# Three batches' roots and normalised tiles of the first attention on GpSimd, its bias additions two pairs later

## The chip, the cores and the metric

The kernel runs on one core of a Trainium2 chip. A core has five engines with a queue each, which meet only through semaphores: TensorE (PE) multiplies, VectorE (DVE) and ScalarE (ACT) read and write PSUM and SBUF, GpSimd (POOL) works on SBUF alone, and SyncE (SP) issues most transfers. The metric is the device time of one execution in microseconds, the median of the runs.

## What is computed

The reference is two transformer layers, each an attention and a feed-forward part with a layer norm after each. The change lies in the first attention, which has 4 batches of 512 rows and 256 columns, 16 heads of 16 columns, and in the norm behind it:

```python
B, S, H = hidden_states.shape
qkv = jnp.einsum('bsh,hf->bsf', hidden_states, w_qkv) + b_qkv
...
q_rot = q_rot * cos + _rotate_half(q_rot) * sin
k_rot = k_rot * cos + _rotate_half(k_rot) * sin
...
scores = jnp.einsum('bhqd,bhkd->bhqk', q, k)
scores = jnp.where(causal, scores, jnp.float32(-jnp.inf).astype(scores.dtype))
probs = jax.nn.softmax(scores, axis=-1)
attn = jnp.einsum('bhqk,bhkd->bhqd', probs, v)
...
return jnp.einsum('bsh,hf->bsf', attn, w_out) + b_out
```

```python
x = _layernorm(x + _L0_attn_ref(x, L0_attn_w_qkv, L0_attn_b_qkv, L0_attn_w_out, L0_attn_b_out), axis=-1)
```

`_layernorm` subtracts the row's mean and divides by the root of its variance plus 1e-5. Everything is float32; products are made of a high and a low part of each operand.

## The kernel before

`attention0` holds one program for each engine. Batches come one after the other in *entries*: `entry(0, "first")`, two of `"loop"` (i = 1, 2) and `entry(3, "last")`. An entry has 8 *pairs* of heads (p = 0 to 7) with 4 *rows of tiles* each (r = 0 to 3), so 32 slots (p, r). Entry i works on the heads of batch i; beside that it prepares the heads of batch i + 1 and finishes batch i - 1: it projects its output, adds the residual, normalises the sum and transposes the result for the next stage. Nothing is scheduled by a planner. The order of each engine is written by hand in tables of slots: `WORK_AT` (the uses of one PSUM bank, `work`), `HIGH_AT` and `LOW_AT` (the high and low parts of the stacked heads), `VALUES_AT`, `BIAS_TILE_AT` and `KEEP_TILE_AT`.

In a slot (p, r) of a loop entry:

- TensorE makes the score products from which row maxima are taken, two pairs ahead (`max_pass`, L824, of 128 (r + 1) columns), the score products for the exponentials (L835), in half of the slots a group of value products (`value_pass`, L848), and one use of the work bank: a projection (L871), a turn of stacked heads (`turn_stack`, L878), a part of the output projection (L887) or a transpose (L943). `max_pass` has two banks; each product waits until VectorE has reduced what was in its bank two products ago.
- VectorE reduces both `max_pass` banks (L1104), adds the bias to projections (L1153), and does the rest of the PSUM reading that falls to it. The norm of batch i - 1 is a generator, `normalise`, of which two steps are taken in each slot from (4, 0): statistics (L86, L91) in (4, 0), nine steps of a root by iteration on 128x4 numbers (L96 to L121), and behind them in (5, 1), all at once, the four tiles `xn = (rsum - mean) * y` (L158).
- ScalarE makes the exponentials (L695), copies turned heads from PSUM (L682, L688) and makes the high parts of stacks (`stack_high`, L674 and L676).
- GpSimd clears the upper triangle of the exponentials (`select`, L579), rotates projected heads (`rotate`, L564 to L568), copies values (L572), and makes the low parts of stacks (`stack_low`, L585 and L587). It adds the output bias to the residual tiles of batch i (`residual_bias`, L606, four tiles at (5, 1), (5, 2), (5, 3), (6, 0)) and keeps the normalised tiles plus a bias (`keep`, L599, four tiles at (6, 2) to (7, 1)).

GpSimd takes its work strictly in this order: in one slot `stack_low`, `select`, `rotate`, `values`, `keep`, `residual_bias`. The turns of stacked heads on TensorE wait for `stack_low`; two of them are in pair 5: half 2, tile 2 at (5, 1), whose low part is made at (5, 0), and half 2, tile 3 at (5, 3), whose low part is made at the head of (5, 3). The latter's heads are rotated at (5, 0). The normalised tiles are first read by the transposes at (6, 2) and by `keep` there; the residual tiles with their bias by the additions at (3, 0) of the next entry.

The last entry has no `rotate`, and no stacks of half 2. It projects nothing for a next batch; its slots have the products of two weight matrices instead (L923, L929), and VectorE has their preparation.

A root of the same kind is already worked out on GpSimd, in the next stage (`pool_rstd`, L135 to L146, called at L1657): twelve operations, each behind a wait for the one before.

Of the kernel before, what the change touches and what calls it, by code (L numbers as in the profile page):

```python
# [127 lines left out]

def pool_rstd(pool, chain, mv, var, t, u, y):

    def step(ins):
# [4 lines left out]
    step(pool.tensor_scalar(y.bitcast(I32), var[:, :].bitcast(I32), -0.5, float(RSQRT_MAGIC), ALU.mult, ALU.add))
    step(pool.tensor_tensor(t[:, :], y, y, ALU.mult))
    step(pool.tensor_tensor(t[:, :], t[:, :], var[:, :], ALU.mult))
    step(pool.tensor_scalar(t[:, :], t[:, :], -1.0, STEP_2[1], ALU.mult, ALU.add))
    step(pool.tensor_tensor(y, y, t[:, :], ALU.mult))  # L140
    step(pool.tensor_tensor(t[:, :], y, y, ALU.mult))
    step(pool.tensor_tensor(t[:, :], t[:, :], var[:, :], ALU.mult))
    step(pool.tensor_scalar(u[:, :], t[:, :], STEP_3_T, None, ALU.subtract))
    step(pool.tensor_tensor(t[:, :], t[:, :], u[:, :], ALU.mult))
    step(pool.tensor_scalar(t[:, :], t[:, :], STEP_2[0] ** 4, 5.0, ALU.mult, ALU.add))
    step(pool.tensor_tensor(y, y, t[:, :], ALU.mult))  # L146
# [146 lines left out]
BIAS_TILE_AT = ((5, 1), (5, 2), (5, 3), (6, 0))  # L293
# [67 lines left out]
def attention0(nc, A, g, top):  # L361
# [444 lines left out]
    def _(pe):  # L806
# [85 lines left out]
        def use_work(i, when, kind, arg):  # L892
# [38 lines left out]
            else:  # L931
# [7 lines left out]
                else:  # L939
                    pe.wait_ge(s["v_norm"], i + 1)  # L940
# [128 lines left out]
    def _(v):  # L1069
        chain = Chain(v, s["v_chain"])  # L1070
        for name in ("work_read", "ex_read", "a_out", "v_norm", "g_x1"):
            v.sem_inc(s[name], 1)
# [179 lines left out]
        def entry(i, when):  # L1252
# [4 lines left out]
            for n, (p, r) in enumerate(slots):  # L1257
# [28 lines left out]
                if (p, r) == (4, 0) and when != "first":  # L1286
                    norm = normalise(i, when)
# [1365 lines left out]
```

## Time and profile before

| | us |
|---|---|
| median of 3 runs | 1067.95 (1067.92 to 1068.65) |
| span of the profiled execution, first to last instruction | 1067.0 |
| TensorE busy | 1004.4 |
| VectorE busy | 747.8 |
| ScalarE busy | 612.4 |
| GpSimd busy | 375.2 |
| first attention: second entry, pair 0 to pair 7 | 97.0 to 161.8 |
| first attention: third entry | 161.8 to 226.6 |
| first attention: last entry | 226.6 to about 307 |

The two loop entries take 64.8 us each and are alike almost to the hundredth: what is seen in the second entry is found again 64.8 us later. "Busy" of TensorE is the time in which a matmul is under way, and matmuls overlap, so that a short idle time of TensorE in a row is more than it looks. In a row of a timeline the number in brackets is the time for which the engine stood idle before it, with what ended it. "PEclk" is the granted TensorE clock as a share of 2.4 GHz: 0.50 is 1.2 GHz.

### The profile page before, as it was taken

The page shows a single profiled execution, that of the slowest core. Times are in us where ns is not written, and L with a number is a line of the kernel's source. Part 1 is how long each engine was busy: PE and PEld are TensorE (multiplying, and loading weights), DVE is VectorE, ACT ScalarE, POOL GpSimd, SP SyncE. Part 2 cuts the span into 40 slices and gives each one's busy share as a digit, 9 for nine tenths or more (in the row PEclk, how much of TensorE's full clock was granted, in tenths as well). Part 3 has the DMA queues.
Part 4 walks back from the last instruction along what each step waited for, and adds up shares of the span by engine and source line. Part 5 has one row for each costly group of instructions (what it writes and reads, how often), then busy time and mean ns, then how long its engine had stood idle before and what let it go on. Part 6 is the DMA issues. An engine that isn't in the chain of part 4 may idle for free.

```text
span 1067.0 us, 18308 instructions
## 1 busy us (share of the span) xinstructions
PE 1004.4 (94%) x6627; PEld 836.8 (78%) x6627; DVE 747.8 (70%) x2042; ACT 612.4 (57%) x1177; POOL 375.2 (35%) x725
## 2 busy tenths in 40 slices
PE   6999999999998898889999999999999999999995
PEld 5555556556667897778989999998999999899995
DVE  5666777777639778967557767666776766677646
ACT  5566667664368576545556665455666545566640
POOL 3444464562121474454622233222223322222600
PEclk9899999999999899999999999999999999999998
DMA  7000000022210001021201010010101001010101
GB/s 244 25 2 21 3 22 21 23 60 80 61 46 4 1 6 36 1 100 61 79 1 40 1 40 22 19 41 1 40 1 41 27 14 40 1 41 1 49 32 40
DMA packets 29234, 36.91 MB, mean 35 GB/s; under 512 B 1780, under 2 KB 26584, under 8 KB 29144
## 3 DMA queue, kind: packets, MB, share of 16 engines
q1 hardware_dynamic: 24872, 31.28, 9.2%
q10 hardware_dynamic: 4272, 4.46, 1.4%
q8 instruction: 53, 0.87, 0.3%
q14 instruction: 37, 0.30, 0.1%
HBM read 31.40 MB, written 4.20 MB: 33 GB/s over the span
## 4 chain that ended last, share of the span: by engine, by line
PE 54%; DVE 5%; ACT 1%; POOL 1%; issue 1%; DMA 1%; SPq 0%; DVEq 0%; POOLq 0%; ACTq 0%
PE ps L1894 25%; PE ps L1877 24%; PE ps L1849 2%; PE ps L1767 1%; PE ps L1818 1%; DVE ln_stats L86 1%; DMA mlp_b<-L_ffn_LN_B 1%; DVE ln_stats L2256 0%; ACT xn L2016 0%; ACT x_b L2037 0%; DVE att L2339 0%; PE ps L1809 0%; DVE xT_l L2298 0%; PE ps L1720 0%; DVE ln_mv L91 0%
## 5 line engine op out<-in xcount | busy, mean ns | idle before, releaser
L2115 ACT ACTIVATE G<-ps,bias_col 128x512 f32<-128x512 f32 x192 | 135.5, 706 | 186.3 <-PE ps L1877 176.8
L1894 PE MATMUL ps<-w_h,G_h 128*128 128x256 f32 x736 | 208.2, 283 | 0.0
L1894 PE MATMUL ps<-w_h,G_l 128*128 128x256 f32 x736 | 207.9, 282 | 0.0
L1894 PE MATMUL ps<-w_l,G_h 128*128 128x256 f32 x736 | 207.8, 282 | 0.0
L2387 DVE TENSOR_TENSOR G_l<-G,G_h 128x512 fp32r<-128x512 f32 x192 | 155.1, 814 | 60.0 <-ACT G_h L2116 60.0
L1696 POOL TENSOR_TENSOR x_a<-xn,mlp_g 128x1024 f32<-128x1024 f32 x20 | 67.6, 3378 | 344.7 <-DVE xn L2417 344.7
L695 ACT ACTIVATE probs<-ps 128x512 f32<-128x512 f32 (+3 forms) x256 | 98.3, 440 | 108.4 <-PE ps L835 108.0
L1877 PE MATMUL ps<-xT_h,w_h 128*128 128x512 f32 x384 | 152.0, 396 | 1.1 <-issue 1.1
L1877 PE MATMUL ps<-xT_h,w_l 128*128 128x512 f32 x384 | 150.6, 392 | 0.0
L1877 PE MATMUL ps<-xT_l,w_h 128*128 128x512 f32 x384 | 150.3, 391 | 0.0
L1894 PEld LDWEIGHTS ps<-w_h,G_h 128*128 128x128 f32 x736 | 139.9, 190 | 0.7
L1894 PEld LDWEIGHTS ps<-w_h,G_l 128*128 128x128 f32 x736 | 140.3, 191 | 0.0
L1894 PEld LDWEIGHTS ps<-w_l,G_h 128*128 128x128 f32 x736 | 139.5, 190 | 0.8
L1104 DVE CUSTOM_DVE_ANT_0 ps<-ps,q_mask 128x128 f32<-128x128 f32 (+3 forms) x256 | 120.5, 511 | 25.9 <-PE ps L824 24.3
L2116 ACT ACTIVATE G_h<-ps,bias_col 128x512 fp32r<-128x512 f32 x192 | 135.0, 703 | 0.0
L2401 DVE TENSOR_TENSOR rsum<-ps,x_a 128x1024 f32<-128x1024 f32 x23 | 28.2, 1225 | 105.5 <-PE ps L1894 105.5
L579 POOL TENSOR_SCALAR_AFFINE_SELECT probs<-probs 128x256 f32<-128x256 f32 x128 | 54.8, 428 | 103.8 <-ACT probs L695 103.6
L1877 PEld LDWEIGHTS ps<-xT_h,w_h 128*128 128x128 f32 x384 | 72.1, 188 | 16.2 <-issue 1.5
L1877 PEld LDWEIGHTS ps<-xT_h,w_l 128*128 128x128 f32 x384 | 72.1, 188 | 15.6
L1877 PEld LDWEIGHTS ps<-xT_l,w_h 128*128 128x128 f32 x384 | 72.2, 188 | 15.0
L824 PE MATMUL ps<-heads_T 64*128 64x128 f32 (+3 forms) x256 | 69.5, 420 | 9.8 <-DVE top_score L1104 8.9
L2381 DVE TENSOR_TENSOR xT_l<-hs,xT_h 128x512 fp32r<-128x512 f32 x40 | 77.0, 1952 | 2.3 <-ACT xT_h L2101 1.2
(303 smaller groups left out, 2125.0 us busy)
## 6 DMA issues: line engine op xcount, KB each, us to landing
w_raw<-L_ffn_W_T SPq DMA_DIRECT2D x12, 1024.0 KB, 5.2
hs<-L_attn_hidden_states SPq DMA_DIRECT2D x8, 512.0 KB, 4.1
x_kept<-hs SPq DMA_DIRECT2D x4, 512.0 KB, 3.2
w_raw<-x_kept SPq DMA_DIRECT2D x2, 1024.0 KB, 5.4
out<-xn SPq DMA_DIRECT2D x3, 512.0 KB, 2.9
w_raw<-L_ffn_ent_w_T SPq DMA_DIRECT2D x1, 1024.0 KB, 10.3
w_raw<-L_ffn_ent_pw SPq DMA_DIRECT2D x1, 1024.0 KB, 12.7
heads_T<-neg_rows SPq DMA_DIRECT2D x64, 2.0 KB
```

Of the source, the lines that this page charges most:

```text
L579: pool.affine_select(diagonal, diagonal, [[0, 2], [1, P]], ALU.is_ge, 0.0, base=0, channel_multiplier=-1).then_inc(s["g_sel"], 1)
L695: act.activation(probs[:, p % 2, o, OFF[j]:OFF[j] + COLS[j]], ps[:, score_bank(r, o), 0:COLS[j]], ACT.Exp).then_inc(s["a_exp"], 1)
L824: pe.matmul(ps[:, o, 0:(t + 1) * P], heads_T[rows, p // UP, 0, p % UP, t * P:(t + 1) * P], heads_T[rows, p // UP, 1, p % UP, 0:(t + 1) * P ...
L1104: v.tensor_tensor_reduce(ps[:, o, 0:(t + 1) * P], ps[:, o, 0:(t + 1) * P], q_mask[:, S - (t + 1) * P:S], 1.0, MASKED, ALU.add, ALU.max, to ...
L1696: pool.tensor_tensor(g.x_a[:, rows, :], xn[:, b % 2, :, :], bcast(g.mlp_g[:, i, :], 1, [P, RT, D]), ALU.mult).then_inc(feed["g_mul"], 1)
L1877: mm = pe.matmul(ps[:, hidden_bank(i, n), :], w[:, c, f * P:(f + 1) * P], x[:, b, c, :], start=(k == 0), stop=(k == 5))
L1894: mm = pe.matmul(ps[:, 4 + t // 2, (t % 2) * D:(t % 2 + 1) * D], x[b % 2][f][:, t * P:(t + 1) * P], w2_chunk(w, f), start=(k == 0), stop=( ...
L2115: act.activation(G32[n % 4], bank, ACT.Gelu, bias=bias)
L2116: act.activation(G_h[b % 2][f], bank, ACT.Gelu, bias=bias).then_inc(feed["a_g"], 1)
L2381: v.tensor_tensor(g.xT_l[:, b, c, :], src, g.xT_h[:, b, c, :].bitcast(F32), ALU.subtract).then_inc(feed["v_T"], 1)
L2387: v.tensor_tensor(G_l[b % 2][f], G32[n % 4], G_h[b % 2][f].bitcast(F32), ALU.subtract).then_inc(feed["v_gl"], 1)
L2401: v.tensor_tensor(g.rsum[:, :, :], ps[:, 4:6, :].rearrange("p a (b c) -> p (a b) c", c=D), g.x_a[:, b * RT:(b + 1) * RT, :], ALU.add).then ...
```

## The change

The root and the four tiles of batches 0, 1 and 2 move from VectorE to GpSimd. VectorE's generator is left with the statistics (`moments`), whose end is told by a semaphore of its own, `v_moments`. GpSimd takes four of the twelve root operations in each of (4, 1), (4, 2), (4, 3), behind `select` and ahead of `rotate`, and one tile in each slot of pair 5. The four bias tiles move from (5, 1), (5, 2), (5, 3), (6, 0) to (6, 0), (6, 1), (7, 2), (7, 3). The semaphore of the finished tiles is named `x1_normed` in place of `v_norm`; its waits stand where they stood. The norm of batch 3, after the last entry, stays on VectorE.

```diff
+POOL_ROOT_STEPS = 12
+def pool_rstd_steps(pool, chain, mv, var, t, u, y):
+    chain.step(pool.tensor_scalar(var[:, :], mv[:, :, 1], EPS, VAR_FACTOR, ALU.add, ALU.mult))
+    yield
+    chain.settle()
+    chain.step(pool.tensor_scalar(y.bitcast(I32), var[:, :].bitcast(I32), -0.5, float(RSQRT_MAGIC),
+                                  ALU.mult, ALU.add))
+    yield
...
 def pool_rstd(pool, chain, mv, var, t, u, y):
+    for _ in pool_rstd_steps(pool, chain, mv, var, t, u, y):
         chain.settle()
...
-BIAS_TILE_AT = ((5, 1), (5, 2), (5, 3), (6, 0))
+BIAS_TILE_AT = ((6, 0), (6, 1), (7, 2), (7, 3))
+ROOT_AT = ((4, 1), (4, 2), (4, 3))
+NORM_TILE_AT = ((5, 0), (5, 1), (5, 2), (5, 3))
...
+        def x1_root(i):
+            pool.wait_ge(s["v_moments"], i)
+            yield from pool_rstd_steps(pool, chain, g.lnw["mv"], g.lnw["var"], g.lnw["t"], g.factors[:, 0, 0, :],
+                                       g.lnw["y"][:, :])
+        def x1_tile(i, t):
+            if t == 0:
+                chain.settle()
+                wait(pool, s["a_nT"], KC * (i - 1))
+            ins = pool.tensor_scalar(xn[:, 0, t, :], g.rsum[:, t, :], g.lnw["mv"][:, t, 0:1], g.lnw["y"][:, t:t + 1],
+                                     ALU.subtract, ALU.mult)
+            if t == RT - 1:
+                ins.then_inc(s["x1_normed"], 1)
...
                     select(i, p, r)
+                    if when != "first" and (p, r) in ROOT_AT:
+                        for _ in range(POOL_ROOT_STEPS // len(ROOT_AT)):
+                            next(root)
+                    if when != "first" and (p, r) in NORM_TILE_AT:
+                        x1_tile(i, NORM_TILE_AT.index((p, r)))
...
-        def normalise(i, when):
...
+        def moments(i, when):
+            v.wait_ge(s["work_read"], WORK.number(i, when, ("out", 1)) + 1)
...
+                ins = v.bn_aggr(g.lnw["mv"][:, k, :], g.lnw["stats"][:, k, :])
+            ins.then_inc(s["v_moments"], 1)
```

VectorE, second entry, slots (5, 1) and (5, 2), before (L1104 are the reductions of the maxima, L121 the last step of the root, L158 the tiles):

```order
L1104 ISA ps,top_score<-ps,q_mask 128x256 [waits p_max]
L1104 ISA top_score 128x1
L1104 ISA ps,top_score<-ps,q_mask 128x256 [waits p_max]
L1104 ISA top_score 128x1
L121 SCALAR_TENSOR_TENSOR ln_y<-ln_t,ln_y 128x4 [waits v_chain]
L158 TENSOR_SCALAR xn<-rsum,ln_mv,ln_y 128x256 [waits g_x1,v_chain]
L158 TENSOR_SCALAR xn<-rsum,ln_mv,ln_y 128x256 x3
L1104 ISA ps,top_score<-ps,q_mask 128x384 [waits p_max]
```

The same place now (L1156 are the reductions):

```order
L1156 ISA ps,top_score<-ps,q_mask 128x256 [waits p_max]
L1156 ISA top_score 128x1
L1156 ISA ps,top_score<-ps,q_mask 128x256 [waits p_max]
L1156 ISA top_score 128x1
L1156 ISA ps,top_score<-ps,q_mask 128x384 [waits p_max]
```

Nothing stands between the reductions of (5, 1) and those of (5, 2) any more; nine small steps and four tiles are gone from slots (4, 1) to (5, 1).

GpSimd, second entry, from the end of (5, 0) to the low parts at the head of (5, 3), before (`val` is the copy of values, `hs` the residual tiles):

```order
L572 COPY val<-qkv 128x8x16
L579 AFFINE_SELECT probs<-probs 128x2x128 [waits a_exp]
L606 TENSOR_TENSOR hs<-hs,b_out 128x256 [waits xres_in]
L579 AFFINE_SELECT probs<-probs 128x2x128 [waits a_exp]
L572 COPY val<-qkv 128x8x16
L606 TENSOR_TENSOR hs<-hs,b_out 128x256
L585 TENSOR_TENSOR q_stack<-qkv,q_stack 128x8x16 [waits a_stack]
L587 TENSOR_TENSOR k_stack<-qkv,k_stack 128x8x16
```

Now, from the tile of (5, 0):

```order
L651 TENSOR_SCALAR xn<-rsum,ln_mv,ln_y 128x256 [waits g_chain]
L594 TENSOR_TENSOR turned<-qkv,rope 128x64 [waits g_rope,work_read]
L595 TENSOR_TENSOR turned<-qkv,rope 128x16x2
L596 TENSOR_TENSOR turned<-qkv,rope 128x16x2
L598 TENSOR_TENSOR qkv<-turned 128x8x2x4 [waits g_chain]
L602 COPY val<-qkv 128x8x16
L609 AFFINE_SELECT probs<-probs 128x2x128 [waits a_exp]
L651 TENSOR_SCALAR xn<-rsum,ln_mv,ln_y 128x256
L609 AFFINE_SELECT probs<-probs 128x2x128 [waits a_exp]
L651 TENSOR_SCALAR xn<-rsum,ln_mv,ln_y 128x256
L602 COPY val<-qkv 128x8x16
L615 TENSOR_TENSOR q_stack<-qkv,q_stack 128x8x16 [waits a_stack]
```

A tile of the norm stands in place of each of the two bias tiles, and one more stands ahead of the rotation of (5, 0).

GpSimd, second entry, slots (4, 1) and (4, 2), now:

```order
L609 AFFINE_SELECT probs<-probs 128x2x128 [waits a_exp]
L134 TENSOR_SCALAR ln_var<-ln_mv 128x4 [waits v_moments]
L137 TENSOR_SCALAR ln_y<-ln_var 128x4 [waits g_chain]
L141 TENSOR_TENSOR ln_t<-ln_y 128x4 [waits g_chain]
L144 TENSOR_TENSOR ln_t<-ln_t,ln_var 128x4 [waits g_chain]
L594 TENSOR_TENSOR turned<-qkv,rope 128x64 [waits g_rope,work_read]
L595 TENSOR_TENSOR turned<-qkv,rope 128x16x2
L596 TENSOR_TENSOR turned<-qkv,rope 128x16x2
L598 TENSOR_TENSOR qkv<-turned 128x8x2x4 [waits g_chain]
L609 AFFINE_SELECT probs<-probs 128x2x128 [waits a_exp]
L147 TENSOR_SCALAR ln_t<-ln_t 128x4 [waits g_chain]
L150 TENSOR_TENSOR ln_y<-ln_y,ln_t 128x4 [waits g_chain]
```

Before, the rotation followed `select` at once, and nothing but a `select` stood in (4, 2). TensorE, ScalarE and SyncE issue the same instructions in the same order as before.

## Rows read from the trace of the kernel before

**Rows 1.** Waits, 130 to 146 us: who waited for whom, total us, times, longest.

```profile
PEld ps L824 <- DVE top_score L1104: 3.1, 5, 1.9
PE ps L824 <- DVE top_score L1104: 1.0, 1, 1.0
```

**Rows 2.** Timeline of TensorE, first entry (start us, us, instruction, idle before).

```profile
68.00 0.39 PE L824 MATMUL ps<-heads_T 64*128 64x256 f32 x2
...
74.01 0.33 PE L824 MATMUL ps<-heads_T 64*128 64x128 f32 x2
...
76.52 0.54 PE L878 MATMUL ps<-ident_r,k_stack 128*128 128x128 f32 x4
...
80.70 0.50 PE L878 MATMUL ps<-ident_r,k_stack 128*128 128x128 f32 x4 [0.58 <-POOL k_stack L587]
...
81.48 0.33 PE L824 MATMUL ps<-heads_T 64*128 64x128 f32 x2
...
84.05 0.39 PE L824 MATMUL ps<-heads_T 64*128 64x256 f32 x2
```

**Rows 3.** Timeline of TensorE, the same slots of the second entry.

```profile
130.23 0.38 PE L824 MATMUL ps<-heads_T 64*128 64x256 f32 x2
...
136.25 0.41 PE L824 MATMUL ps<-heads_T 64*128 64x128 f32 x2
...
138.97 0.51 PE L878 MATMUL ps<-ident_r,k_stack 128*128 128x128 f32 x4
...
142.88 1.01 PE L824 MATMUL ps<-heads_T 64*128 64x512 f32 x2 [0.99 <-DVE top_score L1104]
...
144.29 0.54 PE L878 MATMUL ps<-ident_r,k_stack 128*128 128x128 f32 x4
...
145.09 0.47 PE L824 MATMUL ps<-heads_T 64*128 64x128 f32 x2
...
149.19 0.39 PE L824 MATMUL ps<-heads_T 64*128 64x256 f32 x2
```

**Rows 4.** Timeline of VectorE, second entry, slot (5, 1).

```profile
140.30 2.00 DVE L158 TENSOR_SCALAR xn<-rsum,ln_mv,ln_y 128x256 f32<-128x256 f32 x4
```

**Rows 5.** Busy time by stretch: us, PE, PEld, DVE, ACT, POOL, PEclk, DMA share, GB/s.

```profile
141.70:145.10 3.40, 2.40 (x26) 1.38 (x22) 3.29 (x11) 1.47 (x5) 2.63 (x7) 1.00 0.00 0
145.10:148.50 3.40, 3.40 (x16) 1.72 (x16) 0.63 (x5) 1.94 (x4) 1.10 (x2) 0.50 0.01 2
```

**Rows 6.** Waits of GpSimd, 131.9 to 143.0 us.

```profile
POOL probs L579 <- ACT probs L695: 2.0, 3, 1.4
...
POOL turned L564 <- DVE qkv L1153: 0.7, 2, 0.4
```

**Rows 7.** Timeline of GpSimd, second entry, slots (5, 2) and (5, 3).

```profile
142.41 0.72 POOL L606 TENSOR_TENSOR hs<-hs,b_out 128x256 f32<-128x256 f32 x1
143.09 0.46 POOL L585 TENSOR_TENSOR q_stack<-qkv,q_stack 128x128 fp32r<-128x128 f32 x1
143.50 0.46 POOL L587 TENSOR_TENSOR k_stack<-qkv,k_stack 128x128 fp32r<-128x128 f32 x1
```

**Rows 8.** GpSimd, single lines (minimum/median/maximum ns); then groups, 300 to 560 us.

```profile
L137 POOL TENSOR_TENSOR norm_t<-norm_scale x19: 197/199/702, 354.8 to 511.3; 128x4 f32<-128x4 f32 x19
L1668 POOL TENSOR_SCALAR hs<-rsum,norm_scale,norm_shift x16: 556/564/1606, 469.0 to 521.0; 128x256 f32<-128x256 f32 x16
...
L1668 POOL TENSOR_SCALAR hs<-rsum,norm_scale,norm_shift 128x256 f32<-128x256 f32 x16 | 12.7, 808 | 0.7 <-POOL norm_shift L1660 0.7
...
L138 POOL TENSOR_TENSOR norm_t<-norm_t,norm_var 128x4 f32<-128x4 f32 x19 | 4.7, 246 | 1.5
```

**Rows 9.** Last entry: TensorE in its timeline; then GpSimd's waits, 269 to 293 us.

```profile
260.50 0.62 PE L824 MATMUL ps<-heads_T 64*128 64x512 f32 x2
...
290.59 1.02 PE L824 MATMUL ps<-heads_T 64*128 64x512 f32 x2 [1.12 <-DVE top_score L1104]
...
POOL probs L579 <- ACT probs L695: 23.2, 7, 4.9
```

More of the change, by code:

```diff
@@ L126 @@
 STEP_3_T = 10.0 / (3.0 * STEP_2[0] ** 2)
+POOL_ROOT_STEPS = 12
[7 more added lines that the diff above has]
+    chain.settle()
+    chain.step(pool.tensor_tensor(t[:, :], y, y, ALU.mult))
+    yield
+    chain.settle()
+    chain.step(pool.tensor_tensor(t[:, :], t[:, :], var[:, :], ALU.mult))
+    yield
+    chain.settle()
+    chain.step(pool.tensor_scalar(t[:, :], t[:, :], -1.0, STEP_2[1], ALU.mult, ALU.add))
+    yield
+    chain.settle()
+    chain.step(pool.tensor_tensor(y, y, t[:, :], ALU.mult))
+    yield
+    chain.settle()
+    chain.step(pool.tensor_tensor(t[:, :], y, y, ALU.mult))
+    yield
+    chain.settle()
+    chain.step(pool.tensor_tensor(t[:, :], t[:, :], var[:, :], ALU.mult))
+    yield
+    chain.settle()
+    chain.step(pool.tensor_scalar(u[:, :], t[:, :], STEP_3_T, None, ALU.subtract))
+    yield
+    chain.settle()
+    chain.step(pool.tensor_tensor(t[:, :], t[:, :], u[:, :], ALU.mult))
+    yield
+    chain.settle()
+    chain.step(pool.tensor_scalar(t[:, :], t[:, :], STEP_2[0] ** 4, 5.0, ALU.mult, ALU.add))
+    yield
+    chain.settle()
+    chain.step(pool.tensor_tensor(y, y, t[:, :], ALU.mult))
+    yield
@@ L139, in pool_rstd @@
[L139 to L146, printed above, removed]
@@ L1238, in prepare, with normalise_last @@
                 yield
-        def normalise(i, when):
-            if when == "after":
-                v.wait_ge(s["v_tail"], 2 * KC)
-            else:
-                v.wait_ge(s["work_read"], WORK.number(i, when, ("out", 1)) + 1)
-            yield from layernorm_steps(v, chain, g.lnw, g.rsum, xn[:, 0, :, :], s["v_norm"],
-                                       (s["g_x1"], i))
+        def moments(i, when):
+            v.wait_ge(s["work_read"], WORK.number(i, when, ("out", 1)) + 1)
+            for k in range(RT):
+                ins = v.bn_stats(g.lnw["stats"][:, k, :], g.rsum[:, k, :])
+            chain.step(ins)
+            yield
+            chain.settle()
+            for k in range(RT):
+                ins = v.bn_aggr(g.lnw["mv"][:, k, :], g.lnw["stats"][:, k, :])
+            ins.then_inc(s["v_moments"], 1)
+            yield
+        def normalise_last():
+            v.wait_ge(s["v_tail"], 2 * KC)
+            layernorm(v, chain, g.lnw, g.rsum, xn[:, 0, :, :], s["x1_normed"], (s["g_x1"], B))
         PREPARE_AT = ((1, 2), (1, 3), (2, 0), (2, 1), (2, 2), (2, 3), (3, 2), (3, 3), (4, 0), (5, 1), (5, 3), (6, 1),
@@ L1286, in entry @@
                 if (p, r) == (4, 0) and when != "first":
-                    norm = normalise(i, when)
+                    norm = moments(i, when)
                 next(norm, None)
@@ L1363, in _ @@
                             x_res[:, 2 * half:2 * half + 2, :], ALU.add).then_inc(s["v_tail"], 1)
-        for _ in normalise(B, "after"):
-            pass
+        normalise_last()
         square(v, g, chain, 0)
```

22 lines of the change are left out of this document (9 added, 13 removed).

## The prediction

> **What bounds the kernel now.** The change touches only the first attention, so I read that stage, and first its waits [rows 1]. Between 130 and 146 us, pairs 4 and 5 of the second entry, TensorE's largest wait is for VectorE's maxima: its weight loads stand for 3.1 us, and the matmuls themselves for 1.0 us at one place. Then I read the timelines. The first entry does the same pairs without a norm on VectorE and without bias tiles on GpSimd, so it is the control for both. Pair 4 takes 6.01 us there, from 68.00 to 74.01 [rows 2], and 6.02 us in the second entry, from 130.23 to 136.25 [rows 3]: the root's small steps on VectorE cost nothing there. Pair 5 takes 7.47 us there, from 74.01 to 81.48 [rows 2], and 8.84 us here, from 136.25 to 145.09 [rows 3]: 1.37 us more. That is where the four tiles run in one piece of 2.00 us [rows 4], with the reductions of (5, 2) behind them and TensorE's next product behind those, idle for 0.99 us at 142.88 [rows 3].
>
> More follows. In the 3.4 us of that idle time TensorE is busy for 2.40 us, and in the next 3.4 us its granted clock is 0.50, that is 1.2 GHz [rows 5]. Slot (6, 0) then takes 4.10 us, from 145.09 to 149.19 [rows 3], against 2.57 us in the first entry [rows 2]: 1.53 us for the clock. So up to 2.9 us per loop entry hang on the tiles' place. The third entry repeats all of this.
>
> The rows to read next are those of the engine that gets the work. In the first entry, with VectorE free, TensorE still waits 0.58 us for GpSimd's low part at (5, 3), the row at 80.70 [rows 2]. GpSimd has no slack at that point even without norm or bias. In the second entry the same turn starts at 144.29 [rows 3], and its low part is done at 143.96 (143.50 plus 0.46) [rows 7]: 0.33 us to spare, and only because TensorE is late.
>
> **The change part by part, loop entries.** VectorE loses nine small steps and four tiles; the statistics stay. By the control that is worth 1.37 us of pair 5, if nothing takes its place.
>
> GpSimd gains, ahead of the low part of (5, 3): twelve root steps and three tiles (5, 0) to (5, 2), less the two bias tiles that leave (5, 1) and (5, 2). A step on 128x4 numbers has a median of 0.20 us [rows 8]. Each stands behind a wait for the one before, 0.08 us (1.5 us of idle time over 19, in the row of L138) [rows 8]; in groups of four that wait is met 9 times. 12 x 0.20 + 9 x 0.08 = 3.1 us. A tile of this form on GpSimd has a median of 0.56 us [rows 8], so three are 1.7 us; two bias tiles at 0.72 [rows 7] are 1.4 us. Together 3.4 us more work. Against it stands the time in which GpSimd waits on this stretch: 2.0 us for exponentials and 0.7 us for projections, 2.7 us [rows 6]. All of these waits can be filled, since what they wait for doesn't depend on GpSimd's lateness by a us. The remainder is 0.7 us. Independent neighbours overlap a little: two low parts of 0.46 us start 0.41 us apart [rows 7]; some six added instructions of that kind take 0.3 us off. So the low part ends 0.4 to 0.7 us later, at 144.3 to 144.6, the turn follows by about 0.1 us, and TensorE is at (5, 3)'s turn 0.1 to 0.4 us **later** than before, not earlier. The low part of (5, 1) is late in the same way, with all twelve root steps ahead of it; that wait lies within the later one and is not added. I take +0.2 us: nearer to the overlapped end, because most of GpSimd's rows show such overlap. The wait for the maxima goes, and the wait for GpSimd is what comes next; the 1.37 us are not gained.
>
> TensorE's idle time doesn't go away either, it moves: the pair would run in 7.5 us and takes 9.0. So I take the stretch at half clock to stay, 0 for it; the other end is -1.5 us per entry.
>
> What lies behind pair 5: the last tile is issued in (5, 3), some 0.6 us behind a `select`, and the transposes that need it are two and a half slots later, so they don't wait: 0. The bias tiles add one each to (6, 1), (7, 2) and (7, 3), 0.7 us each. No one waits for them before (3, 0) of the next entry, and behind them in GpSimd's queue are `select`s, whose value products come two slots later, and the low part at (7, 3); I count 0. Without that cover the last one would cost its 0.7 us. No DMA is moved, and SyncE's queue is as before. TensorE's new wait has ScalarE and VectorE behind it, which then have less to do. Two loop entries: 2 x 0.2 = +0.4 us.
>
> **Last entry.** It has no rotations and no stacks of half 2, and its slots are long: GpSimd waits 23.2 us for exponentials between 269 and 293 us [rows 9]. The root and tiles fit into that several times over, and no low part hangs on them. TensorE's idle time of 1.12 us at 290.59 goes [rows 9], and with it the stretching of the two products there, 1.02 us against 0.62 us for the same form at 260.50 [rows 9]: 1.5 us. VectorE's next piece, a weight matrix, may keep back a tenth or two. I take -1.4 us, between 0 (if ScalarE's exponentials hold the end of the entry) and -1.5.
>
> **Sum.** +0.4 - 1.4 = -1.0 us. The profiled span of 1067.0 us becomes 1066.0. The runs' median stands 0.95 us above the span of the profiled execution, which lies around it, and that is kept: **1067.0 us**, 0.1% below 1067.95.
>
> **Rivals.** (a) *GpSimd keeps up* and each loop entry falls to the control: -2 x 1.37 - 1.4 = -4.1 us, 1063.8 us, and with both half-clock stretches gone 1060.8 us. For it: GpSimd is busy only about half the time of the stage. Against it: the 0.58 us at 80.70 without any of this work [rows 2].
>
> (b) *The clock*: GpSimd takes over the bound as forecast, but the idle time, now split between (5, 1) and (5, 3), no longer brings the fall to 1.2 GHz in one entry or in both. -1.0 - 1.5 = -2.5 us, 1065.4 us, or 1063.9 us. Against it: the idle time at (5, 3) should be over the 0.99 us that came with the fall before.
>
> (c) *GpSimd's instructions run longer among VectorE's*, and the kernel gets slower. In the next stage the tile's mean is 0.81 us against a median of 0.56, and a step's 0.25 against 0.20 [rows 8]. At the means a loop entry gets 3 x 0.25 + 12 x 0.05 = 1.3 us longer, all of it on the path, as GpSimd has no slack left: 2 x 1.5 - 1.4 = +1.6 us, 1069.6 us. If the longer wait also brings a second stretch at half clock, +1.5 us more each, 1071 to 1072.6 us. It turns the sign once a loop entry loses more than 0.7 us.
>
> The Trainium skill speaks for (c): its page GPSIMD Engine Reference, section 8. Key points, holds that "for elementwise work, the DVE is structurally ~2× faster" and that GpSimd contends for SBUF with VectorE instructions of two SBUF inputs. By it a tile would take about 1.0 us here, 1.3 us more per loop entry, and the time would come out near that of (c). The trace disagrees in size: 2.00 us for four on VectorE [rows 4] and a median of 0.56 us for one on GpSimd [rows 8] are a factor of 1.1.
>
> **Chances.** Forecast 0.52 (its own range 1066.2 to 1068.8, with both ends of the loop term and of the last entry); (a) 0.08; (b) 0.20; (c) 0.14; and 0.06 that later stretches at half clock, which shift against the program by a us, add or take one, 1.5 us, more often as a gain here. A measurement tells apart about 0.2%, 2.1 us. Faster by more: (a), (b) and the last case, 0.34. Slower by more: the greater part of (c), 0.12. Between: 0.54. The range from 1063.5 to 1070.0 leaves out the far ends of (a) and (c).
>
> **What would show it.** Right: in the second entry VectorE's reductions of (5, 1) and (5, 2) stand next to each other; TensorE's wait at (5, 3) names GpSimd's `k_stack`, over 1 us long; the start of (6, 0) is within 0.5 us of 145.09; the clock is at 0.50 right behind it; the last entry has no 1.12 us of idle time. Wrong: pair 5 of 7.5 to 8 us in a loop entry means that GpSimd had the room (the count of its free time is at fault); one over 9.7 us, that its steps or tiles cost more than their medians. A clock of 1.00 in (6, 0) is (b).

## The result, and the profile after

The changed kernel takes 1084.42 us, the median of 4 runs (1083.1 to 1084.73), against 1067.93 us for the kernel before, also 4 runs. The ratio is 1.0152, with a 95% interval of 1.0138 to 1.0166: 16.5 us slower. The forecast was 1067.0 us with a range that ended at 1070.0 us, so it was wrong. The profiled execution of after has a span of 1082.7 us, 15.7 us over the 1067.0 us of before, and the account below is made between these two.

**Where the pair's time went.** TensorE's timeline of the second entry answers to [rows 3]. L876 is the product for the maxima, L930 a turn of stacked heads; they were L824 and L878.

```profile
135.06 0.33 PE L876 MATMUL ps<-heads_T 64*128 64x128 f32 x2
...
138.36 0.52 PE L930 MATMUL ps<-ident_r,k_stack 128*128 128x128 f32 x4 [0.86 <-POOL k_stack L617]
...
140.69 0.62 PE L876 MATMUL ps<-heads_T 64*128 64x512 f32 x2
...
145.50 0.50 PE L930 MATMUL ps<-ident_r,k_stack 128*128 128x128 f32 x4 [3.54 <-POOL k_stack L617]
...
146.43 0.47 PE L876 MATMUL ps<-heads_T 64*128 64x128 f32 x2
...
156.88 0.73 PE L876 MATMUL ps<-heads_T 64*128 64x128 f32 x2
```

Pair 5 takes 11.37 us (135.06 to 146.43), where it took 8.84 us. The wait for VectorE's maxima before the 128x512 product is gone: the row at 140.69 has no bracket and takes 0.62 us instead of 1.01 us. In its place TensorE stands idle for 0.86 us at (5, 1) and for 3.54 us at (5, 3), both times for GpSimd's low part. Pair 6 takes 10.45 us (146.43 to 156.88), where it took 9.27 us (145.09 to 154.36). The third entry is the same to a tenth.

GpSimd's timeline of the same place answers to [rows 7]. Two steps of the root in (4, 1) come first, then three tiles (L651) and the low part (L617):

```profile
132.21 0.20 POOL L137 TENSOR_SCALAR ln_y<-ln_var 128x4 int32<-128x4 int32 x1
132.49 0.20 POOL L141 TENSOR_TENSOR ln_t<-ln_y 128x4 f32<-128x4 f32 x1
...
138.57 1.24 POOL L651 TENSOR_SCALAR xn<-rsum,ln_mv,ln_y 128x256 f32<-128x256 f32 x1
...
141.47 1.23 POOL L651 TENSOR_SCALAR xn<-rsum,ln_mv,ln_y 128x256 f32<-128x256 f32 x1
...
143.05 1.22 POOL L651 TENSOR_SCALAR xn<-rsum,ln_mv,ln_y 128x256 f32<-128x256 f32 x1
...
144.89 0.46 POOL L617 TENSOR_TENSOR k_stack<-qkv,k_stack 128x128 fp32r<-128x128 f32 x1
```

The steps of the root are what was forecast, 0.20 us long and 0.28 us apart. The tiles are not: 1.22 to 1.24 us each instead of 0.56 us. The line's own row shows that this doesn't come from the neighbourhood (minimum, median and maximum in ns over all twelve tiles):

```profile
L651 POOL TENSOR_SCALAR xn<-rsum,ln_mv,ln_y x12: 1223/1226/1622, 138.6 to 297.7; 128x256 f32<-128x256 f32 x12
```

The minimum is 1223 ns and the median 1226 ns, although four of the twelve stand in the last entry, where VectorE is busy for about half of the time (9.7 of 17.0 us from 285 us on).

**The clock.** Busy time by stretch (columns as in [rows 5]: us, PE, PEld, DVE, ACT, POOL, PEclk and so on):

```profile
143.20:146.60 3.40, 1.10 (x10) 1.02 (x11) 0.00 (x0) 0.57 (x2) 3.40 (x6) 0.90 0.00 0
146.60:150.00 3.40, 3.40 (x16) 1.73 (x17) 0.61 (x4) 1.62 (x4) 0.73 (x2) 0.50 0.00 0
150.00:153.40 3.40, 3.40 (x21) 2.04 (x20) 1.66 (x6) 0.45 (x2) 1.54 (x5) 0.60 0.00 0
```

GpSimd is busy for all of the 3.4 us in which TensorE is busy for 1.10 us. Behind that the clock is at 0.50 as before, and in this execution in most of the next stretch too (0.60, where it was 1.00 before); that is where pair 6 loses its 1.2 us.

**The last entry** did what was forecast. TensorE's product of (5, 2), the first line of [rows 9] with idle time, no longer waits:

```profile
295.70 0.62 PE L876 MATMUL ps<-heads_T 64*128 64x512 f32 x2
```

From the entry's start to this product it takes 62.93 us (232.77 to 295.70), where it took 64.03 us (226.56 to 290.59): 1.10 us less.

**The next stage, where nothing was expected.** A loop entry takes 68.51 us (95.76 to 164.27) instead of 64.81 us, so the three entries give 3.7 + 3.7 - 1.1 = +6.3 us. A stretch at half clock in the first entry (granted clock 0.59 from 60.4 to 63.8 us before, 1.00 now) is absent from this execution: -1.2 us. That leaves 5.1 us of lag at 295.70. The rest comes later. `pool_rstd` works out 19 roots on GpSimd between 350 and 530 us. Its timeline before, one root from its first step to the next root's first step:

```profile
358.25 0.20 POOL L135 TENSOR_SCALAR norm_var<-norm_mv 128x4 f32<-128x4 f32 x1
358.53 0.19 POOL L136 TENSOR_SCALAR norm_scale<-norm_var 128x4 int32<-128x4 int32 x1
358.81 0.20 POOL L137 TENSOR_TENSOR norm_t<-norm_scale 128x4 f32<-128x4 f32 x1
...
362.23 0.20 POOL L135 TENSOR_SCALAR norm_var<-norm_mv 128x4 f32<-128x4 f32 x1
```

and after:

```profile
363.65 0.19 POOL L134 TENSOR_SCALAR norm_var<-norm_mv 128x4 f32<-128x4 f32 x1
364.00 0.20 POOL L137 TENSOR_SCALAR norm_scale<-norm_var 128x4 int32<-128x4 int32 x1 [0.16 <-POOL norm_var L134]
364.35 0.20 POOL L141 TENSOR_TENSOR norm_t<-norm_scale 128x4 f32<-128x4 f32 x1
...
368.40 0.20 POOL L134 TENSOR_SCALAR norm_var<-norm_mv 128x4 f32<-128x4 f32 x1
```

The operations are as long as before, 0.20 us, but stand 0.35 us apart instead of 0.28 us, and a root takes 4.75 us instead of 3.98 us. The code says why: the generator `pool_rstd_steps` waits for the operation before it (`chain.settle()`) ahead of each step, and the loop in the new `pool_rstd` waits for the same operation once more after each `yield`. The second wait is always met already, and it still costs 0.07 us. The third step's row gives the place of the first and the last of the 19 roots; before it was L137 of [rows 8], from 354.8 to 511.3:

```profile
L141 POOL TENSOR_TENSOR norm_t<-norm_scale x19: 199/200/1115, 359.6 to 527.1; 128x4 f32<-128x4 f32 x19
```

The lag is 4.8 us at the first root and 15.8 us at the last: the 19 roots lose 11.0 us, of at most 19 x 0.77 = 14.6 us. Behind them nothing more is lost (15.7 us at the end). ScalarE waits for what GpSimd makes of the root; its waits from 310 to 525 us, before:

```profile
ACT xn L2016 <- POOL norm_shift L1660: 12.7, 6, 5.9
ACT hs L2016 <- POOL norm_shift L1660: 1.7, 5, 0.7
```

and after:

```profile
ACT xn L2076 <- POOL norm_shift L1720: 15.5, 6, 5.4
ACT hs L2076 <- POOL norm_shift L1720: 7.2, 7, 1.4
```

14.4 us have become 22.7 us. The chain that ended last, on the page of after, has GpSimd with 4%; on the page of before it is 1%:

```profile
PE 53%; DVE 5%; POOL 4%; issue 2%; ACT 1%; DMA 1%; POOLq 0%; SPq 0%; DVEq 0%
```

So the trace points to two causes: the doubled wait in `pool_rstd`, 11 us of lag, and the dear tile, which keeps back the low parts in the first attention, some 5 us together with the longer stretch at half clock behind it. Both are read from one trace each; the runs below take them apart.

### The profile page after: what moved, and what is told of

It reads as the page before. It is cut to its first block, busy times and chain, and to the rows that moved or that the text cites. A ratio compares the mean times of both kernels' runs of the same rounds, so it can differ in the third digit from the quotient of the medians.

```text
span 1082.7 us, 18525 instructions
## 1 busy us (share of the span) xinstructions
PE 1008.5 (93%) x6627; PEld 840.3 (78%) x6627; DVE 740.6 (68%) x2003; ACT 612.3 (57%) x1177; POOL 395.9 (37%) x773
## 4 chain that ended last, share of the span: by engine, by line
PE 53%; DVE 5%; POOL 4%; issue 2%; ACT 1%; DMA 1%; POOLq 0%; SPq 0%; DVEq 0%
PE ps L1954 24%; PE ps L1937 24%; PE ps L1827 2%; PE ps L1909 2%; DVE ln_stats L86 1%; DMA mlp_b<-L_ffn_LN_B 1%; ACT xn L2076 1%; PE ps L1878 1%; POOL hs L1728 0%; DVE ln_stats L2316 0%; ACT x_b L2097 0%; POOL norm_var L134 0%; POOL norm_t L153 0%; POOL norm_shift L1720 0%; POOL norm_t L162 0%
## 5 line engine op out<-in xcount | busy, mean ns | idle before, releaser
L1156 DVE CUSTOM_DVE_ANT_0 ps<-ps,q_mask 128x128 f32<-128x128 f32 (+3 forms) x256 | 120.7, 512 | 35.7 <-PE ps L876 34.1
L1937 PEld LDWEIGHTS ps<-xT_h,w_l 128*128 128x128 f32 x384 | 72.3, 188 | 15.7
L876 PE MATMUL ps<-heads_T 64*128 64x128 f32 (+3 forms) x256 | 67.4, 422 | 5.4 <-DVE top_score L1156 4.7
```

What stands on the lines that cost most here:

```text
L876: pe.matmul(ps[:, o, 0:(t + 1) * P], heads_T[rows, p // UP, 0, p % UP, t * P:(t + 1) * P], heads_T[rows, p // UP, 1, p % UP, 0:(t + 1) * P ...
L1156: v.tensor_tensor_reduce(ps[:, o, 0:(t + 1) * P], ps[:, o, 0:(t + 1) * P], q_mask[:, S - (t + 1) * P:S], 1.0, MASKED, ALU.add, ALU.max, to ...
L1937: mm = pe.matmul(ps[:, hidden_bank(i, n), :], w[:, c, f * P:(f + 1) * P], x[:, b, c, :], start=(k == 0), stop=(k == 5))
```

## The experiments

The kernel before was run between the others: 1067.10 us over 22 runs beside the first four experiments, 1067.47 us over 31 runs beside the last four. Its runs go from 1063.5 to 1070.1 us, and the granted clock goes with them, from 0.986 in the fastest to 0.977 or 0.978 in the slowest: stretches at half clock come and go from one execution to the next. Each experiment has one profiled execution, so a difference of a us or two between two profiles need not come from the edit. The ratios stand with their 95% interval; a ratio can differ by 0.1% from that of the two medians. In the first expectations W stands for the doubled wait as what carries most of the loss, and C for the rival by which it lies in the attention.

### One wait for each step

Everything of the change stays; only the loop in `pool_rstd` no longer waits a second time.

```diff
 def pool_rstd(pool, chain, mv, var, t, u, y):
     for _ in pool_rstd_steps(pool, chain, mv, var, t, u, y):
-        chain.settle()
+        pass
+    chain.settle()
```

> The changed kernel with one edit: pool_rstd, the root of the next stage, waits once behind each step again, as before, not twice. In the profile of the changed kernel the starts of its steps are 0.35 us apart where they were 0.28, and the first steps of two successive roots 4.75 us where they were 3.98; behind the first attention the kernel falls back by another 11 us. Theory W (the second wait costs it): 0.77 us per root over the roots that lie on the path gives back 10 to 11 us: 1073 to 1075 us, the step distance 0.28 us again. Rival C (the loss behind the attention comes from the granted clock, because the program is shifted against it, or from the late tiles): 1080 to 1084 us.

Measured: 1071.11 us over 10 runs, ratio 1.0034 [1.0022, 1.0045]. Of the 16.5 us, 12.5 to 13.3 are gone. The stage of the roots is back to its old length (third step, first and last root):

```profile
L141 POOL TENSOR_TENSOR norm_t<-norm_scale x19: 199/200/700, 356.1 to 512.1; 128x4 f32<-128x4 f32 x19
```

156.0 us, where it was 156.5 before and 167.5 in the changed kernel, and ScalarE's waits for that chain are the 12.7 and 1.7 us of before. Pair 5 of the attention is as slow as in the changed kernel, TensorE at (5, 3) of the second entry:

```profile
145.85 0.50 PE L931 MATMUL ps<-ident_r,k_stack 128*128 128x128 f32 x4 [3.54 <-POOL k_stack L618]
...
146.67 0.47 PE L877 MATMUL ps<-heads_T 64*128 64x128 f32 x2
```

Pair 6 is not as slow: it takes 9.17 us (146.67 to 155.84) and 9.57 us in the third entry, instead of 10.45 and 10.37 us, because the clock is back earlier (1.00 from 150.1 to 153.5 us, 0.90 in the stretch that answers to it in the third entry). The code of the attention is the same, so the longer stretch at half clock belongs to the one execution and not surely to the change. The three entries cost +2.25, +3.03 and -1.56 us against before, together +3.7 us; the runs give 4.0 us by the medians (1071.11 - 1067.10) and 3.6 us by the ratio. That is W's side, but 2 to 4 us below the 1073 to 1075 us that W expected: the attention's shorter time, 2.1 us in the loop entries and 0.5 us in the last, accounts for most of that.

### The second wait alone, in the kernel before

```diff
 def pool_rstd(pool, chain, mv, var, t, u, y):
     def step(ins):
         chain.step(ins)
         chain.settle()
+        chain.settle()
```

> The kernel before with that one part of the change alone: a second wait, already fulfilled, behind each of the 12 steps of pool_rstd. Theory W: the time goes up by the same 10 to 11 us, to 1078 to 1079 us, and the step distance to 0.35 us, with nothing changed in the first attention. Rival C: no change, 1067 to 1070 us.

Measured: 1077.81 us over 4 runs, ratio 1.0095 [1.0077, 1.0113]: 10 to 11 us for a wait that is always met. The third step's row, and then ScalarE's waits from 310 to 525 us, show the same from the other side:

```profile
L138 POOL TENSOR_TENSOR norm_t<-norm_scale x19: 199/199/1114, 353.1 to 521.1; 128x4 f32<-128x4 f32 x19
```

```profile
ACT xn L2017 <- POOL norm_shift L1661: 15.8, 6, 5.5
ACT hs L2017 <- POOL norm_shift L1661: 6.0, 6, 1.4
```

168.0 us from the first root to the last, 11.5 us more than before, and ScalarE's waits are 21.8 us, near the 22.7 us of the changed kernel. With this the doubled wait is shown both ways, by removal from after and by addition to before.

### What makes the tile dear

Eighteen operations on 128x256 numbers, three of each form, are added to the kernel before on GpSimd, near its start, where VectorE is busy for 6.2 of 19.0 us; they write a buffer that is overwritten before it is used.

```diff
+        one, two, src, dst = rope[:, 0, 0, 0:1], rope[:, 0, 1, 0:1], x_res[:, 0, :], att[:, 0, :]
...
+        for _ in range(3):
+            chain.step(pool.tensor_scalar(dst, src, one, two, ALU.subtract, ALU.mult))
+            chain.settle()
+        for _ in range(3):
+            chain.step(pool.tensor_scalar(dst, src, one, two, ALU.mult, ALU.add))
+            chain.settle()
...
```

> The kernel before with eighteen extra GpSimd instructions ahead of the first entry, three of each of six forms on one 128x256 tile, each behind a wait for the one before, writing a tile that is not yet in use: (x - p) * q, x * p + q, x * p - q, (x + p) * q with p, q columns of SBUF; (x - 0.5) * 2 with constants; x - p alone. The output stays the reference's. Theory F (the pair of operations sets the price): (x - p) * q takes 1.22 us as in the changed kernel, x * p + q 0.56 us as in the next stage; the others tell which part is dear. Rival S (VectorE's traffic or the place in the first attention makes the tiles slow): all forms take about the same time here, 0.56 or 1.22 us.

The six forms, in this order: (x - p) * q, x * p + q, x * p - q, (x + p) * q, (x - 0.5) * 2 with constants, and x - p alone:

```profile
L646 POOL TENSOR_SCALAR att<-hs,rope x3: 1219/1232/1247, 31.8 to 34.5; 128x256 f32<-128x256 f32 x3
...
L649 POOL TENSOR_SCALAR att<-hs,rope x3: 554/554/556, 35.8 to 37.1; 128x256 f32<-128x256 f32 x3
...
L652 POOL TENSOR_SCALAR att<-hs,rope x3: 1218/1218/1229, 37.7 to 40.4; 128x256 f32<-128x256 f32 x3
...
L655 POOL TENSOR_SCALAR att<-hs,rope x3: 554/558/559, 41.7 to 43.0; 128x256 f32<-128x256 f32 x3
...
L658 POOL TENSOR_SCALAR att<-hs x3: 1068/1070/1081, 43.7 to 46.0; 128x256 f32<-128x256 f32 x3
...
L661 POOL TENSOR_SCALAR att<-hs,rope x3: 917/922/924, 47.2 to 49.2; 128x256 f32<-128x256 f32 x3
```

The subtraction is what costs: 1.22 to 1.23 us with it, 0.55 us without, in either place of the pair, 1.07 us with two constants, and 0.92 us even where it is the only operation. An addition in its place costs nothing. The tile of the change is the first form; the row that the forecast took for it, L1668 of [rows 8], is the second. The kernel's own time, 1078.3 us in one run, holds the 18 added operations and is no measure of anything else.

### The change with a cheap tile

The same normalised tile written without a subtraction: `rsum * y + (-mean * y)`. Two more steps on 128x4 numbers work out the second factor, behind the root.

```diff
+            chain.settle()
+            chain.step(pool.tensor_tensor(g.factors[:, 1, 0, :], g.lnw["mv"][:, :, 0], g.lnw["y"][:, :], ALU.mult))
+            chain.settle()
+            chain.step(pool.tensor_scalar(g.factors[:, 1, 0, :], g.factors[:, 1, 0, :], -1.0, None, ALU.mult))
+            yield
...
-            ins = pool.tensor_scalar(xn[:, 0, t, :], g.rsum[:, t, :], g.lnw["mv"][:, t, 0:1], g.lnw["y"][:, t:t + 1],
-                                     ALU.subtract, ALU.mult)
+            ins = pool.tensor_scalar(xn[:, 0, t, :], g.rsum[:, t, :], g.lnw["y"][:, t:t + 1], g.factors[:, 1, 0, t:t + 1],
+                                     ALU.mult, ALU.add)
```

> The changed kernel with the single wait in pool_rstd, and with its tiles on GpSimd written as rsum * y + (-mean * y), the form that took 0.55 us alone, in place of (rsum - mean) * y, which took 1.22 us. It needs two more steps on 128x4 numbers, in (5, 0). Theory F (the form of the tile is what the prediction mis-sized, the rest of its sum holds): three tiles at 0.56 us and fourteen steps make the low part of (5, 3) 0.5 us later than the prediction had it; pair 5 of a loop entry takes 9.2 to 9.7 us (11.3 us in the changed kernel), the last entry is 1.5 us shorter, and the time is 1066 to 1068.5 us beside 1067.1 us for the kernel before. Rival C (GpSimd's instructions also run longer among VectorE's in this stage): tiles of 0.8 us or more in the profile and 1069.5 us or more.

Measured: 1068.51 us over 12 runs, ratio 1.0014 [1.0000, 1.0027], with the single wait as well. GpSimd and TensorE in the second entry:

```profile
143.10 0.56 POOL L657 TENSOR_SCALAR xn<-rsum,ln_y,norm_factors 128x256 f32<-128x256 f32 x1
144.27 0.45 POOL L618 TENSOR_TENSOR k_stack<-qkv,k_stack 128x128 fp32r<-128x128 f32 x1
...
144.87 0.72 PE L938 MATMUL ps<-ident_r,k_stack 128*128 128x128 f32 x4 [2.20 <-POOL k_stack L618]
...
146.03 0.47 PE L884 MATMUL ps<-heads_T 64*128 64x128 f32 x2
```

The tiles take the 0.56 us of the forecast, at the same places where the dear form took 1.23 us. From the pair's start (135.85) to the low part's are 8.42 us; before it was 7.25 us (136.25 to 143.50). The forecast's 0.4 to 0.7 us, and 0.56 us for the two added steps, make 1.0 to 1.3 us, and 1.17 us are measured. But the pair takes 10.18 us (in the third entry 9.78 us) where 9.0 us and the same 0.56 us would have made 9.6 us, in part because the clock already falls within it: the turn at 144.87 takes 0.72 us instead of 0.50 us. Both lie above the 9.2 to 9.7 us that were expected of this run, and its time is at the upper end of the expected range. This is the nearest run to what was forecast, and it is no gain either.

### VectorE keeps the work, but not in one piece

The kernel before, with VectorE's four tiles in four slots, (5, 1), (5, 2), (5, 3) and (6, 0), instead of all in (5, 1). If the clustering is what costs, as the forecast's control says, this gains without GpSimd.

```diff
+            for k in range(RT):
+                ins = v.tensor_scalar(xn[:, 0, k, :], g.rsum[:, k, :], g.lnw["mv"][:, k, 0:1], y[:, k:k + 1],
+                                      ALU.subtract, ALU.mult)
...
+                yield
+                if k:
+                    yield
```

> The kernel before, root and tiles on VectorE as they were, but the four tiles of batches 0 to 2 one to a slot, (5, 1), (5, 2), (5, 3), (6, 0), not all four in (5, 1). Theory L (the piece of 2.0 us makes TensorE late, not VectorE's sum of work): TensorE's idle time of 0.99 us at (5, 3) goes, pair 5 of a loop entry takes 7.6 to 8.2 us instead of 8.84, the last entry gains 1 us: 1064 to 1066 us, or 1061 to 1063 us if the stretch at half clock behind it goes too. Rival T (VectorE's total work in the pair bounds it): pair 5 stays at 8.8 us and the time within 0.1% of 1067.9 us.

Measured: 1064.59 us over 12 runs, ratio 0.9973 [0.9962, 0.9985]. The execution that was profiled is the slowest of the twelve (1070.66 us), so the gain can't be read from its trace. The wait for the maxima is gone in both loop entries, and GpSimd's low part takes over, in the third entry:

```profile
210.31 0.50 PE L878 MATMUL ps<-ident_r,k_stack 128*128 128x128 f32 x4 [1.29 <-POOL k_stack L587]
...
211.08 0.33 PE L824 MATMUL ps<-heads_T 64*128 64x128 f32 x2
```

Pair 5 takes 8.63 us there (202.45 to 211.08) instead of 8.84 us. In the second entry TensorE waits 1.26 us at the same place, and the pair takes 9.81 us (136.71 to 146.52), longer than before; a stretch at half clock lies on its start:

```profile
136.40:139.80 3.40, 3.40 (x14) 2.39 (x12) 2.34 (x11) 1.84 (x5) 2.13 (x6) 0.58 0.24 84
```

The time came out as expected, the pair in neither entry as short as the expected 7.6 to 8.2 us. So the sentence of the forecast that GpSimd comes next holds even if GpSimd gets nothing to do; its two bias tiles still stand ahead of the low part, and the version with both, below, shows what they hold back.

### The bias tiles later, alone

```diff
-BIAS_TILE_AT = ((5, 1), (5, 2), (5, 3), (6, 0))
+BIAS_TILE_AT = ((6, 0), (6, 1), (7, 2), (7, 3))
```

> The kernel before with the bias tiles alone moved to (6, 0), (6, 1), (7, 2), (7, 3). Theory V (VectorE's piece in (5, 1) sets pair 5 in the kernel before, and nobody waits for the bias at either place): pair 5 stays at 8.8 us and the time within 0.1% of before. Rival B (the bias tiles delay something behind (7, 3), or already hold pair 5): 1 us or more up or down, with a wait for GpSimd changed in pair 5 or in pair 0 of the next entry.

Measured: 1063.38 us over 10 runs, ratio 0.9973 [0.9956, 0.9989]. VectorE and TensorE of the second entry, against [rows 4] and [rows 3]:

```profile
140.42 1.43 DVE L158 TENSOR_SCALAR xn<-rsum,ln_mv,ln_y 128x256 f32<-128x256 f32 x4
...
142.43 1.01 PE L824 MATMUL ps<-heads_T 64*128 64x512 f32 x2 [0.42 <-DVE top_score L1104]
```

VectorE's four tiles take 1.43 us instead of 2.00 us once no bias tile of GpSimd runs beside them, and TensorE waits 0.42 us instead of 0.99 us. Pair 5 becomes 0.57 us shorter (8.27 us), and the stretch at half clock behind it doesn't come:

```profile
143.60:147.00 3.40, 3.40 (x34) 2.22 (x32) 1.65 (x9) 2.64 (x6) 0.81 (x2) 1.00 0.01 2
```

A loop entry takes 62.65 us instead of 64.81 us. The forecast counted 0 for this part of the change, and theory V, the same count, fell. Rival B had that the bias tiles already hold pair 5, though they do it through VectorE's tiles and not by a wait for GpSimd.

### Both together

VectorE's tiles in four slots, and the bias tiles later (the two diffs above).

> The kernel before with VectorE's four tiles one to a slot, (5, 1) to (6, 0), and GpSimd's bias tiles at (6, 0), (6, 1), (7, 2), (7, 3), as the change has them. With the tiles spread alone TensorE's wait at (5, 3) turned to GpSimd's low part, 1.29 us, which has two bias tiles ahead of it. Theory G (behind VectorE's piece the next bound of pair 5 is GpSimd's queue): without those two, 1.4 us less, that wait is 0 to 0.6 us, as in the first entry, and pair 5 takes 7.5 to 7.9 us: 1061.5 to 1064 us. Rival T (VectorE bounds next): a wait for VectorE takes its place, pair 5 stays at 8.4 us or more, 1064 to 1066 us.

Measured: 1059.98 us over 8 runs, ratio 0.9931 [0.9907, 0.9954], the fastest of all that were run. TensorE and one of VectorE's tiles in the second entry, and then the busy time of the stretch around them:

```profile
142.68 0.50 PE L878 MATMUL ps<-ident_r,k_stack 128*128 128x128 f32 x4 [0.58 <-POOL k_stack L587]
...
143.14 0.41 DVE L1251 TENSOR_SCALAR xn<-rsum,ln_mv,ln_y 128x256 f32<-128x256 f32 x1
...
143.45 0.33 PE L824 MATMUL ps<-heads_T 64*128 64x128 f32 x2
```

```profile
142.80:146.20 3.40, 3.40 (x28) 2.21 (x29) 1.39 (x9) 2.07 (x4) 0.50 (x2) 1.00 0.01 2
```

The wait at (5, 3) is the 0.58 us of the first entry [rows 2], without GpSimd taking anything from VectorE. Pair 5 takes 7.95 us (135.50 to 143.45), pair 6 7.74 us at full clock, a loop entry 62.40 us. The control's 7.47 us are not reached: of the 1.37 us of pair 5, 0.89 us came back, and no run shows what holds the other 0.48 us. The time is also 1.5 us below the expected range. Of the 7.9 us between the two profiled executions, 4.8 us lie in the two loop entries and 0.9 us in the last; the rest lies outside them and was not traced to the edit.

### The root on GpSimd, the tiles on VectorE

The last question is which half of the moved work hurts once the tile's price is known. Root on GpSimd as in the change, with the single wait and the bias tiles late; the tiles on VectorE, one a slot from (5, 1) to (6, 0).

```diff
                     if when != "first" and (p, r) in ROOT_AT:
                         for _ in range(POOL_ROOT_STEPS // len(ROOT_AT)):
                             next(root)
-                    if when != "first" and (p, r) in NORM_TILE_AT:
-                        x1_tile(i, NORM_TILE_AT.index((p, r)))
+                    if when != "first" and (p, r) == ROOT_AT[-1]:
+                        next(root)
...
+            v.wait_ge(s["g_root"], i)
+            v.wait_ge(s["g_x1"], i)
+            for k in range(RT):
+                ins = v.tensor_scalar(xn[:, 0, k, :], g.rsum[:, k, :], g.lnw["mv"][:, k, 0:1], g.lnw["y"][:, k:k + 1],
+                                      ALU.subtract, ALU.mult)
```

> The changed kernel with the single wait, its root on GpSimd in (4, 1) to (4, 3) as it is, but the tiles on VectorE, one to a slot, (5, 1) to (6, 0); the bias tiles late. It separates the root's part from the tiles' part. The prediction's count: GpSimd gets 3.1 us of steps and loses two bias tiles of 1.4 us ahead of the low part of (5, 3), against 2.7 us of waiting, so it has 1 us to spare and the root costs nothing there; VectorE is rid of its steps. Theory G: pair 5 at 7.5 to 7.9 us and 1061 to 1064 us, as e6 or a little better. Rival R (the root alone already delays GpSimd's low parts, at (5, 1) above all): a wait of 0.5 us or more at (5, 1) for k_stack, pair 5 at 8.2 us or more, and a time above that of e6.

Measured: 1063.32 us over 12 runs, ratio 0.9963 [0.9949, 0.9976]: 3.3 us over the version with both, though the two intervals overlap a little (0.9954 and 0.9949). TensorE's two turns of pair 5:

```profile
138.95 0.50 PE L934 MATMUL ps<-ident_r,k_stack 128*128 128x128 f32 x4 [1.10 <-POOL k_stack L618]
...
143.09 0.50 PE L934 MATMUL ps<-ident_r,k_stack 128*128 128x128 f32 x4 [0.73 <-POOL k_stack L618]
```

With VectorE's root there is no wait at (5, 1) at all; with GpSimd's twelve steps it is 1.10 us, and pair 5 takes 8.45 us instead of 7.95 us. That is rival R, and not the count of the forecast, by which the root would cost nothing here. The root alone costs half a us per loop entry on GpSimd, 1.0 us of the 3.3 us; another 1.2 us stand in pair 0 of the last entry, where the clock falls to 0.53 in this execution and not in the other, and can't be laid to the root.

## Why the prediction was wrong, step by step

**What was never in the sum: `pool_rstd`.** The part of the forecast on the change went through the first attention alone. The diff rewrites `pool_rstd` too, the function of the next stage, and the doubled `settle` stands in it. 11.0 of the 15.7 us of span are lost there; the run that adds the wait gives 10 to 11 us, and the run that removes it 11.5 us in the stage of the roots, of the 12.5 to 13.3 us that it gains in all. The trace of the kernel before could have told that this matters: ScalarE waits 14.4 us for that chain. The step that failed is the first one, "The change touches only the first attention".

**The price of a tile.** "A tile of this form on GpSimd has a median of 0.56 us [rows 8]" is wrong in its first words: the row's form is a product and a sum, the tile's a difference and a product, and that costs 1.23 us. Three tiles are 2.0 us more than the sum had, on an engine of which the same paragraph says that it has no slack at that point. With that one price mended the working for the low part of (5, 3) holds: 0.4 to 0.7 us and 2.0 us make 2.4 to 2.7 us; the low part begins 9.83 us into the pair (135.06 to 144.89) instead of 7.25 us, 2.58 us later. The forecast took TensorE's loss at (6, 0) as +0.2 us; mended it is +2.2 us, and +2.53 us are measured.

**The clock.** "So I take the stretch at half clock to stay" holds in kind: it stands behind pair 5 in both loop entries. Its size was off in the profiled execution: most of two such stretches instead of one, +1.2 us per loop entry, which rival (c) had as +1.5 us. With the single wait, where the attention has the same code, pair 6 is 0.1 us shorter than before in one loop entry and 0.3 us longer in the other, so how much of these 2.4 us the change brings in the mean of many executions stays open.

**The bias tiles.** "I count 0": nobody waits for them where they are now, and that held. But that they stood beside VectorE's four tiles, and stretched them from 1.43 to 2.00 us, was not seen. The control had this in its 1.37 us of pair 5, which I gave wholly to VectorE's work; 0.57 us of it were the neighbour's. Its control for pair 4, "6.01 us there" against 6.02 us, covers the slots (4, 1) to (4, 3) alone, from the 64x256 product on; six of the nine steps on VectorE lie there, and for these the conclusion stands.

**What held.** GpSimd has no slack in pair 5 and takes over the bound: the wait at (5, 3) names `k_stack` and is over 1 us long. The cost and number of the root's steps were right. All of GpSimd's waiting between the root's first step and the low part of (5, 3) is filled, as forecast: its only wait there, 1.5 us for ScalarE, comes before the root. The last entry gains 1.1 us of the 1.4 us (1.56 us in the first experiment, 1.28 us with the cheap tile). And the mark set beforehand held, a pair 5 over 9.7 us for steps or tiles above their medians: it takes 11.37 us.

**The rivals.** (a) and (b) fell: pair 5 is far from 7.5 us, and the clock is at 0.50 behind it in both entries. (c) had the right direction with another mechanism: not contention with VectorE, since the form takes 1.23 us near the start of the kernel too and the cheap form 0.56 us at the same places, but the operation itself. What the runs show of contention goes the other way: GpSimd's bias tiles stretched VectorE's tiles. The Trainium skill's rule that was weighed (GPSIMD Engine Reference, 8. Key points, VectorE about twice as fast on elementwise work) gave an estimate of 1.0 us for a tile. One tile takes VectorE 0.41 us in the fastest version and GpSimd 1.23 us, a factor of three, so the trace went the rule's way and beyond it; the forecast had set it aside with a row of another form. That form, a product and a sum, is 0.55 us on GpSimd, a factor of 1.3 against VectorE's tile.

**The size of the range.** The forecast lies 17.4 us below what was measured, and 16.7 us below by the spans (+15.7 instead of -1.0). What was left out (11.0) and what was mis-sized (4.0 for the tiles, 2.4 for the clock, over two entries) make 17.4 us; that this is the very difference of the times is luck. The rest of the span's account is smaller: +0.6 us because a loop entry loses 0.3 us more at (6, 0) than the mended term, +0.3 us because the last entry gains less, -1.2 us for the stretch at half clock that is absent from the first entry, and -0.4 us by which the lag shrinks behind the attention, outside the roots. Together that makes the 16.7 us. The range held none of it: its upper end was made of rival (c) alone, and no case stood for a piece of the diff that the sum hadn't priced.

## What to carry to other kernels

- Where a diff rewrites a helper, look for all its callers, and price the helper's new form at each. A wait that is always met is not free in a chain of tiny operations: 0.07 us on each of 12 steps of 19 roots made the kernel before 1% slower.
- A price must come from a row with the same operations, not only with the same shape and engine. If there is none, the ends of the range are as far apart as the nearest forms.
- Before work is moved to an engine that the next wait already names, try to spread it where it is, and to clear what stands beside it. Here that gives 0.7% (1059.98 us), and the move by itself gives nothing even with its two faults mended (1.0014 [1.0000, 1.0027]).
- When one profiled execution is compared with another, look where in the spread of the runs each lies. Here stretches at half clock of more than a us came and went with no edit near them.

## What the runs showed of the hardware

- On GpSimd a `tensor_scalar` over 128x256 float32, with factors for each partition, takes 0.55 us as product and sum, or as sum and product, and 1.22 us as soon as one of the two is a subtraction; with two constants 1.07 us, with the subtraction alone 0.92 us.
- A second wait on a semaphore that has already reached its value costs GpSimd 0.07 us (steps on 128x4 numbers 0.35 us apart instead of 0.28 us).
- A `tensor_tensor` of GpSimd on 128x256 numbers beside four of VectorE's tiles stretches these from 1.43 to 2.00 us. One of VectorE's tiles by itself, without a bias tile beside it, is 0.41 us.
- Removing 0.57 us of TensorE's idle time in a pair also removed the stretch at 1.2 GHz behind it, and that was worth more than the idle time itself: 2.16 us per loop entry in all, and the same in both (bias tiles later, alone).
